# Scores of the second stage from high and low parts, one key unit moved

## The reference

```
x = x + self_attention(layernorm(x))          # 16 heads of 32, causal, alibi, rational softmax
x = x + cross_attention(layernorm(x), ctx)    # 8 heads of 64; ctx: 16 x 750 x 384, a mask per key
x = x + experts(layernorm(x))                 # 8 experts, top 2, hidden 2048
```

## Time and profile before

| | us |
|---|---|
| median of 3 runs (3229.1 to 3232.17) | 3229.51 |
| the profiled execution | 3229.13 |
| its span, first to last instruction | 3227.3 |
| TensorE busy | 3018.3 (94%) |
| VectorE busy | 1646.6 (51%) |
| ScalarE busy | 1348.0 (42%) |
| GpSimd busy | 700.2 (22%) |
| L1487, scores, 1024 instructions, busy | 196.9 |

### The profile page before, as it was taken

The page is one execution under the profiler, slowest core; times in us unless marked ns, Lnnn a source line. Parts: engine busy times, 40 slices in busy tenths (PEclk is TensorE's granted clock), DMA queues, the critical chain, the costliest instruction groups (busy, mean ns, idle before and its releaser), DMA issues. The chain is left out here.

```text
span 3227.3 us, 50841 instructions
## 1 busy us (share of the span) xinstructions
PE 3018.3 (94%) x19312; PEld 2477.8 (77%) x19312; DVE 1646.6 (51%) x3608; ACT 1348.0 (42%) x2298; POOL 700.2 (22%) x721
## 2 busy tenths in 40 slices
PE   5889998978999999999999949999999999999997
PEld 4667777756788777778777738888888888888886
DVE  5888888873556556666566633333333333333321
ACT  5677777764555555555555511111111111111111
POOL 0000000011111221112121033243434343434332
PEclk9889999989999999999999969999999999999999
DMA  3011111123111111111111022141313131313122
GB/s 100 24 35 44 37 45 45 46 82 121 42 50 38 45 38 56 51 38 42 41 52 34 25 74 75 54 97 55 96 55 96 56 95 56 95 57 94 57 71 37
DMA packets 93875, 189.72 MB, mean 59 GB/s; under 512 B 17568, under 2 KB 27552, under 8 KB 91712
## 3 DMA queue, kind: packets, MB, share of 16 engines
q1 hardware_dynamic: 79168, 158.68, 16.1%
q0 software_dynamic: 14592, 29.43, 5.1%
HBM read 140.25 MB, written 47.82 MB: 58 GB/s over the span
## 5 line engine op out<-in xcount | busy, mean ns | idle before, releaser
L1777 ACT ACTIVATE f_hf<-f_h 128x448 f32<-128x448 f32 x256 | 139.4, 544 | 1014.1 <-PE f_h L1804 958.0
L1748 DVE CAST f_hh<-f_hf 128x448 fp32r<-128x448 f32 x256 | 105.9, 414 | 847.0 <-ACT f_hf L1777 822.0
L1819 PE MATMUL f_y<-f_w2h,f_hh 128*128 128x512 f32 x896 | 357.5, 399 | 0.0
L1819 PE MATMUL f_y<-f_w2h,f_hl 128*128 128x512 f32 x896 | 354.0, 395 | 0.0
L1819 PE MATMUL f_y<-f_w2l,f_hh 128*128 128x512 f32 x896 | 352.2, 393 | 0.0
L1707 POOL TENSOR_TENSOR f_w1l<-f_raw,f_w1h 128x512 fp32r<-128x512 f32 x128 | 182.4, 1425 | 778.6 <-DVE f_w1h L1731 778.5
L1396 ACT ACTIVATE c_s_sb<-c_s_sb,c_nmx 112x750 f32<-112x750 f32 x256 | 236.1, 922 | 159.6 <-DVE c_nmx L1239 156.6
L1388 ACT COPY c_pT<-psum 125x672 f32<-125x672 f32 x256 | 184.6, 721 | 224.3 <-PE psum L1496 223.2
L1804 PE MATMUL f_h<-f_xTh,f_w1h 128*128 128x448 f32 x1024 | 255.2, 371 | 2.9 <-DVE f_xTl L1736 1.4
L1496 PEld LDWEIGHTS psum<-a_ident,c_s_sb 112*125 112x125 f32 x1536 | 193.5, 189 | 79.9 <-issue 76.2
L1804 PE MATMUL f_h<-f_xTl,f_w1h 128*128 128x448 f32 x1024 | 250.7, 366 | 0.0
(11 more groups left out here) (252 smaller groups left out, 5766.6 us busy)
## 6 DMA issues: line engine op xcount, KB each, us to landing
f_raw<-in_w SPq DMA_DIRECT2D x128, 512.0 KB, 4.2
h_craw<-in_ctxT SPq DMA_DIRECT2D x16, 1125.0 KB, 5.1
a_x_in<-in_x SPq DMA_DIRECT2D x9, 896.0 KB, 5.5
a_xr<-in_x SPq DMA_DIRECT2D x8, 896.0 KB, 6.0
x_dram<-a_xr SPq DMA_DIRECT2D x8, 896.0 KB, 4.8
q_dram<-a_q SPq DMA_DIRECT2D x32, 224.0 KB, 5.4
h_q<-q_dram SPq DMA_DIRECT2D x16, 448.0 KB, 5.4
c_x<-x_dram SPq DMA_DIRECT2D x16, 448.0 KB, 4.9
```

Of the source, the lines that this page charges most:

```text
L1748: dve.tensor_copy(hs[0][:, l % 2, c * HC:c * HC + HC], hf[:, c, :]).then_inc(h_hi, 1)
L1777: act.activation(hf[:, c, :], H[:, 0:HC], ACT.Gelu_apprx_tanh).then_inc(free, 1)
L1819: mm = pe.matmul(Y[t][:], hs[a][:, l % 2, 128 * t:128 * t + 128], w2s[b][:, l % NSLOT, :], start=j == 0 and q == 0, stop=last_of_expert(l) ...
```

## The change

- `scores`: from the second batch on, the product of `q` and `kT` is three `float32r` products summed in PSUM: high x high, high queries x low keys, low queries x high keys. Twelve calls of `matmul` in place of four. The first batch keeps `q`, `kT` and the float32 product.
- Keys: for a K unit ScalarE's copy out of PSUM now writes the high part and raises `keys_hi`; VectorE then subtracts it from PSUM for the low part (`lo_of_keys`), and only this frees the bank. VectorE does so at the end of step s, after the maxima and before `tail`, for the K units of slots 1 and 2 of step s-1 and of slot 0 of step s; K(3,0) at the end of the batch.
- Queries: ScalarE's copy writes the high part and raises `q_hi`; VectorE makes the low part (`lo_of_queries`) in steps 9 and 15, before `tail`.
- The parts lie in memory where `kT` and `q` did and in two work areas of the first stage.
- K(1,0) moves from step 8 to step 9, between XT(1) and PV(1).

```diff
-            8: ([], [K(1, 0)], [XT(0)]), 9: ([], [XT(1), PV(1)], []), ...
+            8: ([], [], [XT(0)]), 9: ([], [XT(1), K(1, 0), PV(1)], []), ...
@@ VectorE
+        def lo_of_keys(i, kind, unit):
+            dve.wait_ge(keys_hi, number(SPLIT, i, kind, unit) + 1)
+            (hi, lo), src = unit_places(kind, unit)
+            dve.tensor_tensor(lo, src, hi.bitcast(F32), ALU.subtract).then_inc(gen_free[BANK[kind, unit]], 1)
+        def lo_of_queries(i, g):
+            dve.wait_ge(q_hi, i * 2 + g - 1)
+            pair = slice(2 * g, 2 * g + 2)
+            dve.tensor_tensor(q_part[1][:, pair], q2[:, pair], q_part[0][:, pair].bitcast(F32), ALU.subtract).then_inc(q_made, 1)
...
                     masked(*step(i, s + 2))
+                for unit in (projections(kind, s - 1, (1, 2)) if s else []) + projections(kind, s, (0,)):
+                    if unit[0] == "K":
+                        lo_of_keys(i, kind, unit)
+                if s in (9, 15) and kind != "last":
+                    lo_of_queries(i + 1, s // 10)
                 if kind != "first":
                     tail(i, kind, s)
+            if kind != "last":
+                lo_of_keys(i, kind, K(3, 0))
@@ ScalarE
-            act.copy(dst, src).then_inc(gen_free[BANK[kind, unit]], 1)
+            if unit[0] == "K":
+                act.copy(dst[0], src).then_inc(keys_hi, 1)
+            else:
+                act.copy(dst, src).then_inc(gen_free[BANK[kind, unit]], 1)
@@ TensorE
-            for a in range(2):
-                for e in range(2):
-                    mm = pe.matmul(scb[e][0:R, a, 0:HW], q[rows, m, t0:t0 + R], kT[rows, m, j0:j0 + HW],
-                                   start=True, stop=True, tile_position=(64 * e, 0))
+            native = isinstance(i, int) and i == 0
+            parts = [(q, kT)] if native else [(q_part[x], kT_part[y]) for x, y in ((0, 0), (0, 1), (1, 0))]
+            for n, (queries, keys) in enumerate(parts):
+                for a in range(2):
+                    for e in range(2):
+                        mm = pe.matmul(scb[e][0:R, a, 0:HW], queries[rows, m, t0:t0 + R], keys[rows, m, j0:j0 + HW],
+                                       start=n == 0, stop=n == len(parts) - 1, tile_position=(64 * e, 0))
```

More of the change, by code:

```diff
@@ L61, in __init__ @@
         self.cT = [sb(f"cT{k}", [128, CC, J], F32R) for k in "hl"]
+        self.kT_over = Region(nc, "c_", sb.at, sb.end)
         self.kT = sb("kT", [128, H2 // 2, J])
@@ L66, in __init__ @@
         sb = self.region("h_", "values")
-        self.q2, self.q = sb("q2", [128, KC, T]), sb("q", [128, KC, T])
+        self.q2 = sb("q2", [128, KC, T])
+        self.q_over = Region(nc, "c_", sb.at, sb.end)
+        self.q = sb("q", [128, KC, T])
         self.pieces = [(w_k, self.wk, k) for k in range(CC)] + [(w_v, self.wv, k) for k in range(CC)] + [(w_o, self.wo, k) for k in range(KC)]
@@ L171, in self_attention @@
     alibi_q = sb("alibi_q", [128, NPAIR], BF16)
+    handover.low = Region(nc, "c_", sb.at, sb.at + 2 * TPI * C * 4)
     xr = sb("xr", [R, TPI, C])
@@ L892, in cross_attention @@
     q2, q, ident = handover.q2, handover.q, handover.ident
+    kT_part = [handover.kT_over("kT_hi", [128, H2 // 2, J], F32R)[:], handover.low("kT_lo", [128, H2 // 2, J], F32R)[:]]
+    q_part = [handover.q_over("q_hi", [128, KC, T], F32R)[:], handover.low("q_lo", [128, KC, T], F32R)[:]]
     sb = handover.consts
@@ L961, in cross_attention @@
             4: ([], [OUT(1)], []), 5: ([], [PV(0)], []), 6: ([], [K(0, 0)], []), 7: ([], [K(0, 1)], []),
-            8: ([], [K(1, 0)], [XT(0)]), 9: ([], [XT(1), PV(1)], []), 10: ([], [V(0, 0)], [RT]), 11: ([K(1, 1)], [K(2, 0)], []),
+            8: ([], [], [XT(0)]), 9: ([], [XT(1), K(1, 0), PV(1)], []), 10: ([], [V(0, 0)], [RT]), 11: ([K(1, 1)], [K(2, 0)], []),
             12: ([], [V(0, 1)], []), 13: ([], [PV(2)], [PRE]), 14: ([], [V(0, 2)], []), 15: ([K(2, 1)], [K(3, 0)], [])}
@@ L1011, in unit_places @@
         if what == "K":
-            return handover.key_places(bank(kind, unit), m, a)
+            j0, width = (0, KEY_SPLIT) if a == 0 else (KEY_SPLIT, J - KEY_SPLIT)
+            return [part[:, m, j0:j0 + width] for part in kT_part], bank(kind, unit)[:, 0:width]
         return v[:, 2 * a:2 * a + 2, 256 * m:256 * m + 256], bank(kind, unit)[0:JB].rearrange("p (b c) -> p b c", b=2)
@@ L1029, in cross_attention @@
     xn_stored, out_stored = sem("xn_stored"), sem("out_stored")
-    q_made, mb_made = sem("q_made"), sem("mb_made")
+    q_hi, q_made, mb_made, keys_hi = sem("queries_hi"), sem("q_made"), sem("mb_made"), sem("keys_hi")
     gen_full = sem("gen_full")
@@ L1378, in copy_queries @@
             act.wait_ge(q_loaded, i * 16 + 16)
-            act.copy(q[:, 2 * g:2 * g + 2], q2[:, 2 * g:2 * g + 2]).then_inc(q_made, 1)
+            pair = slice(2 * g, 2 * g + 2)
+            if isinstance(i, int) and i == 0:
+                act.copy(q[:, pair], q2[:, pair]).then_inc(q_made, 1)
+            else:
+                act.copy(q_part[0][:, pair], q2[:, pair]).then_inc(q_hi, 1)
         def evacuate(i, kind, unit):
@@ L1482, in scores @@
                 pe.wait_ge(q_made, i * 2 + u // 4 + 1)
-            for a in range(2):
-                for e in range(2):
-                    rows = slice(64 * e, 64 * e + 64)
-                    j0 = a * (J - HW)
-                    mm = pe.matmul(scb[e][0:R, a, 0:HW], q[rows, m, t0:t0 + R], kT[rows, m, j0:j0 + HW],
-                                   start=True, stop=True, tile_position=(64 * e, 0))
+            native = isinstance(i, int) and i == 0
[3 more added lines that the diff above has]
+                    for e in range(2):
+                        rows = slice(64 * e, 64 * e + 64)
+                        j0 = a * (J - HW)
+                        mm = pe.matmul(scb[e][0:R, a, 0:HW], queries[rows, m, t0:t0 + R], keys[rows, m, j0:j0 + HW],
+                                       start=n == 0, stop=n == len(parts) - 1, tile_position=(64 * e, 0))
             mm.then_inc(s_full, 1)
```

## The result

| | before | after |
| --- | --- | --- |
| median of 4 runs, us | 3230.69 (3229.10 to 3232.17) | 3302.77 (3301.76 to 3304.63) |
| profiled execution and its span, us | 3229.13, 3227.3 | 3304.63, 3302.8 |
| granted clock over the span | 0.970 | 0.963 |

The changed kernel is slower by 2.24%: the ratio is 1.0224, with an interval of 1.0206 to 1.0242. The prediction said 3296 us, and its range was 3245 to 3335. One of the three things by which it would be wrong came true all the same: the clock in the middle batches isn't 1.00.

The account below looks back on a forecast made before the run. TensorE was taken as the bound of the second stage, 68.15 us a batch. Shorter scores and added waits summed to +4.56 a batch, +64 over fourteen, +67 with first and last batch: 3229 + 67 = 3296 us, range 3245 to 3335.

Parts of the forecast that it names:

- three things by which it would be wrong: Batch under 68.1 us, scores over 1.45 us, or clock in the middle batches not 1.00.
- The scores at 1.22 us: TensorE's scores call: 1.22 us instead of 1.45, 1.84 less a batch; bounds 0.94 and, if pairs run singly, 2.25.
- Low parts, 0.55 us: VectorE's subtraction: 0.55 us a key unit, 0.62 a query half, 5.6 a batch; costs as order, not as busy time.
- Steps 8 and 9, net +2.1 of waits: TensorE idles before T(8) 0.6, XT(1) 0.25, K(1,0) 0.9, PV(1) 0.95 us; 2.1 more waiting a batch.
- V(0,0), 1.9: Steps 10 and 11: V(0,0) waits 1.9 us for its bank, freed by K(1,0)'s low part behind the masking.
- K(2,0), 1.1: Steps 10 and 11: K(2,0) idles 1.1 us for RT's bank, as K(1,1)'s low part precedes the routing on VectorE.
- V(1,0), 1.6: Steps 15, 0 and 1: V(1,0) waits 1.6 us for the bank that K(3,1)'s low part frees.
- The scores of step 0, -0.3: The 0.3 us these scores waited for the maxima goes, since VectorE's routing no longer delays step 12's masking.
- a rival of mine: The clock falls too: one such place a batch +20 us, two +39, total 3317 to 3336; chance 0.18.
- The first batch, +2.8: First batch keeps f32 scores but has the new order: T(8) about 1 us late, V(0,0) 1.9, about +2.8.
- The last batch, 0: Last batch: seven short scores calls, -1.6 us, against V(1,0)'s wait, +1.6: 0.
- +4.56 a batch: Sum for each of fourteen middle batches, in us: -1.84 + 2.1 + 1.9 + 1.1 + 1.6 - 0.3.

Follow-up runs that it names:

- Written out: Middle batches of the second stage written one after another, without the loop, no order changed; the kernel before so written took 3229.43 us, ratio 0.9995.
- the order alone: Kernel before with only K(1,0) moved from step 8 to step 9, f32 scores, no low parts: 3268.18 us with the loop, 3264.29 without.
- three passes alone: Kernel before with later batches' scores as three one-pass products of the high parts, no low parts, K(1,0) in step 8: 3236.87 us with the loop, 3207.99 without.
- low parts in the old order: Changed kernel with K(1,0) back in step 8, keys' low parts at the end of VectorE's step: 3274.41 us with the loop, 3269.65 without.
- low parts first: Changed kernel, K(1,0) in step 8, VectorE making low parts of step s-1's keys at the beginning of step s: 3271.0 us with the loop, 3254.6 without.
- The GpSimd versions: Changed kernel without the loop, K(1,0) in step 8, GpSimd making the parts from ScalarE's copy: 3235.34 us; with two waits added on GpSimd, 3209.16 us.

## Why the prediction was right

Written out and at clock 1.00, a batch takes: before 67.8, the order alone 69.9, three passes alone 66.3, with low parts in the old order 69.45, low parts first 68.9, the full change 71.8. The change is thus made of +2.1 for the order, -1.5 for the passes and the rest, +3.4, for the low parts, 4.0 a batch; the clock adds to that. The split is not unique: in the old order the low parts add 3.15, and on top of them the order adds 2.35. Step by step:

- *The scores at 1.22 us*: 1.23 start to start at 1136.42, and 1.22 at 1189.31. The one-pass products run in pairs; neither bound, 0.94 or 2.25, came. Of the 1.84 a batch, 1.5 arrives; what holds the other 0.3 was not settled.
- *Low parts, 0.55 us*: 541 ns and 0.63 for the queries (0.62). VectorE at 65%: 63%.
- *Steps 8 and 9, net +2.1 of waits*: the order alone costs 2.1. In the batch at clock 1.00 shown above, T(8), XT(1), K(1,0) and PV(1) start 3.03, 3.81, 5.28 and 7.85 us behind the scores, where the prediction had 2.94, 3.80, 5.15 and 7.75. T(8) 0.52 (0.6), K(1,0) 0.87 (0.9), PV(1) 0.5 on average (0.95), XT(1) nearly nothing (0.25). PV(1) waits 0.73 to 0.76 where K(1,0) is at full clock; at the lower clock K(1,0) is longer and covers the wait.
- *V(0,0), 1.9*: 1.57 by the profile. It starts 3.69 us behind the scores, 3.80 was forecast.
- *K(2,0), 1.1*: 0.79, for L1299, as named.
- *V(1,0), 1.6*: mis-sized. The wait on the low part before V(0,0) is 14 x 1.57 = 22 of the 25.8 us in that group, so some 4 are left for V(1,0), 0.3 a batch. In the loop T(0) ahead of it waits 0.24 to 1.01 us for ScalarE, 0.6 on average, and V(1,0) waits only where that is short; written out, V(1,0) waits 0.79 and T(0) not at all. The two together are 0.8 a batch either way (0.85 with the loop), half of the 1.6. The step of the working that was off: it tied ScalarE's query copy to the scores of step 0 as in the earlier trace rows, to end 1.64 behind them. In the written-out changed kernel it ends 1.10 behind them (scores 998.74, copy 999.29 and 0.55 long), since the maxima before it are read earlier: their negation starts 0.57 ahead of the scores there, and 0.02 ahead in the kernel before.
- *The scores of step 0, -0.3*: too large. The 0.3 of the earlier trace rows is idle time of the weight load. TensorE's last group of K(3,0) starts 0.67 us ahead of the scores in the kernel before and 0.62 in the written-out changed kernel, so about 0.05 was there to win.
- *The clock stays at 1.00*: wrong, and by the prediction's last line this alone makes it wrong. It was a rival of mine with a chance of 0.18, at +20 for one such place in each batch. It came in ten batches of fourteen and cost 13 us. The gaps were as short as the argument against it had said, the longest 1.57 us, and the clock fell all the same.
- *The first batch, +2.8*: 4.7. It is the order: between masks this batch takes 66.3 and 66.8 us in the changed kernel with and without its loop, 66.8 and 66.9 with the order alone, which has no low part, and 61.9 and 62.4 in the kernel before. Where it loses more than forecast was not looked into; TensorE is busy 59.9 us in it instead of 58.1, at 0.91 instead of 0.93, and with nearly the same code for this batch as before the three passes with the loop take 63.9, so that some 2 us are within what one profile can tell. *The last batch, 0*: 0.8 with all behind it.

So that +4.56 a batch comes so near to the measured 4.72 is luck: two errors cancel. At clock 1.00 in the loop the batch is 72.0, +3.85: the sum was 0.7 too high, above all by V(1,0)'s wait; and the clock, which the sum had at nothing, gave 0.9 back. With the measured terms the sum closes: -1.5 for the passes, +2.1 for steps 8 and 9, +1.57, +0.79 and +0.8 are 3.8. The mechanism of the waits is as forecast: the low parts cost by their place in the order, since they stand between a finished product and the release of its bank. Two runs bear on this. With the same work of VectorE in another place in its queue, 0.55 us a batch of the 3.15 goes; with the release taken away from the low part, all of it but 0.3 or so goes (66.71 against 66.42 for the three passes, both as the mean of fourteen batches). The second also moves the work to GpSimd; parts that VectorE makes from a copy in SBUF, behind a bank that is already free, were not tried, and so it is not shown that they are free as work for VectorE.

The loop was in no step of mine. Where it shows: with three passes alone the whole gain of the passes goes (3237 against 3208 written out), in part by T(0)'s wait and in part by the clock, which fell in five batches with the loop and in none without. For the full change it matters little, 72.0 against 71.8 at clock 1.00.

## What to carry to other kernels

When a step is added between a product and the release of its bank, don't price the step; find what stands before it in its engine's queue (and before its input, in the queue of the engine that makes this), and what is the next but one to use the bank. Here 0.54 us of work held TensorE up to 1.6 us behind a masking with which it has nothing to do, and giving the release to the engine that was there already, with the parts made from SBUF by a third engine that was mostly idle, turned +1.2% into -0.7% (both in the old order and written out). The other 1.0% of the loss came with the moved key unit, which costs as much where there is no low part. The third engine is free only where its operations don't lie beside those of VectorE that they slow, so look at mean durations of the neighbours as well as at waits.

## What the runs showed of the hardware that was not expected

- *The turn of a hardware loop on ScalarE.* From the start of its last copy to the start of the first in the next turn it took 1.2, 1.93, 2.65 or 3.40 us, in steps of about 0.73, and the kernel before is mostly at the lowest, the changed one at 1.9 or 2.6. The first two middle batches don't show it: there the copy follows T(15)'s start by 0.94, as it does in every batch when the loop is written out. What the engine does in that time, and what chooses the step, is open.
- *The clock under many short waits.* In the changed kernel no wait in a middle batch is over 1.6 us, TensorE is busy 93%, and the clock fell in ten batches of fourteen; written out, one batch was at 0.91 with nearly the same waits as others at 1.00. The GpSimd versions, idle for 0.9 to 2.4 us a batch (and 3.9 in one), stayed at 1.00; the order alone, 2.3 us idle, and low parts first, 3.3, fell in some batches. In the changed kernel each fall begins within about 1 us after the wait before K(1,0) or after that before V(0,0), in the three passes with a loop behind a wait of 2.1 us before T(0). Idle time per batch alone does not tell which batch falls, and which of the waits tips it was not tried.
- *VectorE beside GpSimd.* With a GpSimd cast or subtraction at the same time, a 112x128 comparison takes 1078 ns instead of 284, a 112x16 product 514 instead of 175, a 112x512 normalisation 928 instead of 545, while the masking from PSUM keeps its 0.93 us. GpSimd's own f32 subtraction of 128x376 takes 0.97 us on average (1.11 beside the comparison, 0.85 at 1172.01 beside nothing), VectorE's from PSUM 0.54.
